# Re-ordering the first batch of an adaptive-norm transformer block: where component weights land, whose statistics come first, and who makes W_out's low parts

## The chip, the cores and the metric

The kernel runs on one core of a Trainium2 chip. The metric is the device time of one execution in microseconds (us), lower is better. The kernel before takes 377.56 us, the median of 3 runs (375.85 to 378.01).

## What is computed

Four batches of 512 tokens with 512 features, all in fp32. A conditioning vector gives six components of modulation; each batch goes through a modulated layer norm, an attention-like step and a feed-forward step. Cut to what matters here:

```
mod = (silu(c) @ wmod).reshape(B, 6, 1, -1)
sa, ca, ga, sb, cb, gb = (mod[:, i] for i in range(6))
ga = (2*(ga >= 0) - 1) * max(|ga|, 0.25)          # gb likewise
h  = layernorm(x) * (1 + ca) + sa
Xn = layernorm(h) * gamma + beta
Q, K, V = split(Xn @ W_in + b_in)
K, V = rotary(K), rotary(V)
A  = 0.5 * sum_over_tokens(cos_sim(K) * cos_sim(V)) + 0.5
x  = x + ga * ((A * Q) @ W_out + b_out + h)
h2 = layernorm(x) * (1 + cb) + sb
x  = x + gb * (relu(h2 @ W_up.T) @ W_down.T + (sum of top-2 softmax) * (h2 @ W_expert))
```

## The kernel before, in words

Every engine has its own program, written out by hand, and runs it strictly in order; semaphores tie them together. Tokens lie in tiles of 128 rows (four per batch, `t` 0 to 3) and features in chunks of 128 (four, `c` or `k`). A matrix product in fp32 accuracy is made of three products of a high part and a low part (`three`, L1175): the high part is a copy in `fp32r`, the low part is the remainder, one subtraction. So every operand has a "hi" copy, mostly on ScalarE (ACT) and a "lo" subtraction, mostly on VectorE (DVE) or GpSimd (POOL).

`PE` (TensorE) computes for batch 0: modulation rows (L1184, L1190), transposes of the normalised tile (`transposes0`, L1213), then `kv_tile(0, t)`: K and V of one row tile, 24 matmuls. Between tiles 1 and 2 stands `mod_rest` (L1196), which computes the other four components from four weight matrices of 1 MB at once, and after tile 2 `mod_turn` (L1207), which transposes them. Then come four feature chunks of Q (`feature_chunk`, twelve matmuls each) with the transposes of batch 1 between them, the four sums `a_sums` (L1259), `kv_tile(1, 0)`, and `out_rows_of(0)` (L1269), the product with W_out, which waits chunk by chunk for Q's low parts `g_lo` (`q_los`). Chunk 1 of Q shares a PSUM bank with the turned components and waits until DVE has read them (`mod_cols`, L1040, semaphore `col_sb`).

DVE carries in batch 0 (`first_attention`, L890): the layer-norm statistics, the bias rows of K and V (`kv_rows`), the rotary products (`kv_products`), the weighted sum over tokens (`kv_sum`), the low parts of the transposed tiles (`t0_split`, `t_split`), the rows `h` of batch 1 (`h_row`), `mod_gates` and `mod_cols`. Where it leaves batch 0 it makes `a_col` and `ab_col` (`a_evac`, L854), for which ACT's scaling of Q (`q_evac`, L603) waits, and after it `q_split` (L861).

ACT squares K and V for the norms (`norm_sums`, L529), normalises rows (`normalise`, `normalise_x`), and evacuates the transposes (`t0_evac`, `t_evac`). `kv_products(b, t)` on DVE waits for ACT's square of K.

POOL raises to the power -0.5 (`power`, `rstd_x`, `rstd_h`), makes low parts of weights (`low_kv`, `low_q`, `out_weight`), multiplies rows (`scale_rows`, L433) and adds the output bias to the rows h of batches 0 and 1 (`base`, L427, eight additions behind batch 0's sums).

`SP` issues every DMA on one queue in order. The weights of K and V come through the two halves of `stage`; a half is free again when its four low parts exist (`wlo_k`, `wlo_v`). The slots of `xs` that batches 2 and 3 will take hold the weights of the first two components at the start. Before, the four later component weights lie so:

```
MODS = ((2, x_slot(2)), (5, gate_bc[:]), (4, stage[:, 0, :]), (3, stage[:, 1, :]))
w_raw = (stage[:, 0, :], stage[:, 1, :], x_slot(3), stage[:, 0, :], stage[:, 1, :], ...)
```

## Time and profile before

| what | value |
|---|---|
| median of 3 runs | 377.56 us (375.85 to 378.01) |
| the profiled execution | 377.15 us, of which the span of the core is 375.1 us |
| PE busy | 353.0 us (94%) |
| DVE busy | 251.0 us (67%) |
| ACT busy | 165.9 us (44%) |
| POOL busy | 125.4 us (33%) |
| chain that ended last | PE 66%, DVE 13%, issue 10%, ACT 5%, POOL 3%, DMA 2% |

The table is an average over very different stages. PE is busy almost without a gap from about 75 us to the end; its idle time lies in the first 75 us, where DVE is busy nearly all the time. A row of the timeline gives the start, the duration of the group, the engine, the line and the operation, and in brackets the idle time before it with what ended it.

### The profile page before, as it was taken

Reading aid. Unit: us, or ns where it says so; the run is one execution under the profiler, and the core shown is the slowest. Engines: PE = TensorE matmul, PEld = TensorE weight load, DVE = VectorE, ACT = ScalarE, POOL = GpSimd, SP = SyncE. Lnnn points to the kernel's source line nnn. Section 1 sums busy time; section 2 is a strip of 40 time slices with the busy share of each in tenths; the row PEclk is TensorE's granted clock in tenths of the full one; section 3 lists DMA queues with packets and bytes.
Section 4 is the critical chain, followed back from the end, with each engine's and each line's share of the span. In section 5 each row is a group of like instructions: output and inputs, shape, how many; then the busy total and the mean of one; then the engine's idle time right before and its main releaser. Section 6 shows DMA issues by size and latency. Waiting matters only on the chain.

```text
span 375.1 us, 4910 instructions
## 1 busy us (share of the span) xinstructions
PE 353.0 (94%) x1776; PEld 287.6 (77%) x1776; DVE 251.0 (67%) x501; ACT 165.9 (44%) x317; POOL 125.4 (33%) x128
## 2 busy tenths in 40 slices
PE   3879797999998999989999999999999999999996
PEld 1238385788887888868888888988998898889885
DVE  2787999856978588885887458436812772383374
ACT  1476957772437811175305691246142604341110
POOL 0285745984932529325163151830010010000000
PEclk9969999989999999999999999999999999999999
DMA  6989567320030000000000002000200020011003
GB/s 199 389 319 315 221 223 243 141 121 2 1 84 0 2 0 16 14 1 2 0 28 2 0 0 114 21 10 28 87 0 0 30 84 2 0 58 57 0 2 113
DMA packets 10968, 27.45 MB, mean 73 GB/s; under 512 B 1200, under 2 KB 1584, under 8 KB 9792
## 3 DMA queue, kind: packets, MB, share of 16 engines
q1 hardware_dynamic: 10944, 27.13, 20.3%
q8 instruction: 14, 0.23, 0.2%
q14 instruction: 10, 0.08, 0.1%
HBM read 22.90 MB, written 4.23 MB: 72 GB/s over the span
## 4 chain that ended last, share of the span: by engine, by line
PE 66%; DVE 13%; issue 10%; ACT 5%; POOL 3%; DMA 2%; SPq 1%; POOLq 0%; DVEq 0%; ACTq 0%
PE ps L1177 21%; PE ps L1179 20%; PE ps L1178 20%; PE ps L1225 2%; DVE hb L771 2%; DMA xs<-in_X 2%; ACT sqj L536 1%; POOL hrs L383 1%; DVE hst L781 1%; ACT ps L599 1%; ACT z L587 1%; ACT t_hi L601 1%; PE ps L1190 1%; DVE prod L827 1%; DVE acc L841 1%
## 5 line engine op out<-in xcount | busy, mean ns | idle before, releaser
L1177 PE MATMUL ps<-wv_hi,t_hi 128*128 128x260 f32 (+1 forms) x192 | 62.2, 324 | 1.0 <-issue 0.6
L1178 PE MATMUL ps<-wv_lo,t_hi 128*128 128x260 f32 (+1 forms) x192 | 61.7, 322 | 0.0
L1179 PE MATMUL ps<-wv_hi,t_lo 128*128 128x260 f32 (+1 forms) x192 | 61.7, 321 | 0.0
L1177 PE MATMUL ps<-t_hi,w_hi 128*128 128x512 f32 x128 | 50.7, 396 | 2.4 <-DVE sb_col L1045 2.4
L1177 PE MATMUL ps<-w_hi,g_hi 128*128 128x512 f32 (+1 forms) x132 | 51.3, 389 | 0.0
L1179 PE MATMUL ps<-w_hi,g_lo 128*128 128x512 f32 (+1 forms) x132 | 50.6, 384 | 0.0
L1178 PE MATMUL ps<-w_lo,g_hi 128*128 128x512 f32 (+1 forms) x132 | 50.6, 383 | 0.0
L1179 PE MATMUL ps<-t_hi,w_lo 128*128 128x512 f32 x128 | 50.0, 391 | 0.0
L1178 PE MATMUL ps<-t_lo,w_hi 128*128 128x512 f32 x128 | 50.0, 390 | 0.0
L1177 PEld LDWEIGHTS ps<-wv_hi,t_hi 128*128 128x128 f32 x192 | 36.3, 189 | 4.8 <-issue 1.7
L1178 PEld LDWEIGHTS ps<-wv_lo,t_hi 128*128 128x128 f32 x192 | 36.4, 189 | 3.1
L1179 PEld LDWEIGHTS ps<-wv_hi,t_lo 128*128 128x128 f32 x192 | 36.4, 189 | 3.0
L383 POOL TENSOR_TENSOR hrs<-hve,expo 128x4 f32<-128x4 f32 (+2 forms) x12 | 11.5, 959 | 77.8 <-DVE hve L788 61.2
L1177 PEld LDWEIGHTS ps<-t_hi,w_hi 128*128 128x128 f32 x128 | 24.1, 188 | 7.6 <-DVE sb_col L1045 2.9
L536 ACT ACTIVATE sqj<-ps 128x512 bf16<-128x512 f32 x16 | 9.5, 593 | 44.8 <-DVE ps L810 37.7
L1177 PEld LDWEIGHTS ps<-w_hi,g_hi 128*128 128x128 f32 x132 | 24.8, 188 | 5.2 <-DVE g_lo L863 0.6
L1179 PEld LDWEIGHTS ps<-w_hi,g_lo 128*128 128x128 f32 x132 | 24.8, 188 | 5.0
L1178 PEld LDWEIGHTS ps<-w_lo,g_hi 128*128 128x128 f32 x132 | 24.8, 188 | 4.7
L354 POOL TENSOR_TENSOR rnm<-nsq,expo 128x2 f32<-128x2 f32 x16 | 11.5, 720 | 49.6 <-ACT sqj L536 49.6
L1179 PEld LDWEIGHTS ps<-t_hi,w_lo 128*128 128x128 f32 x128 | 24.0, 188 | 5.1
L1094 DVE SCALAR_TENSOR_TENSOR g_lo<-ps,g_hi 128x512 fp32r<-128x512 f32 x16 | 11.1, 692 | 24.9 <-ACT g_hi L616 24.8
L1178 PEld LDWEIGHTS ps<-t_lo,w_hi 128*128 128x128 f32 x128 | 24.1, 188 | 4.7
(151 smaller groups left out, 721.9 us busy)
## 6 DMA issues: line engine op xcount, KB each, us to landing
stage<-in_w SPq DMA_DIRECT2D x4, 1024.0 KB, 6.4
out<-xs SPq DMA_DIRECT2D x15, 256.0 KB, 2.0
xs<-in_X SPq DMA_DIRECT2D x3, 1024.0 KB, 9.1
xs<-in_wmod SPq DMA_DIRECT2D x8, 256.0 KB, 5.9
stage<-in_w SPq DMA_DIRECT2D x8, 256.0 KB, 8.2
stage<-in_wmod SPq DMA_DIRECT2D x2, 1024.0 KB, 9.8
gate_bc<-mod_rows SPq DMA_DIRECT2D x8, 256.0 KB, 3.3
xs<-in_X SPq DMA_DIRECT2D x2, 512.0 KB, 6.9
```

The costliest lines, as they stand in the source:

```text
L354: nc.gpsimd.tensor_tensor(dst, src, expo[:, 0:n], ALU.pow).then_inc(s, 1)
L383: nc.gpsimd.tensor_tensor(hrs[:, t0:t0 + n], hve[:, t0:t0 + n], expo[:, 0:n], ALU.pow).then_inc(hrs_s, n)
L536: nc.scalar.activation(sqj[:], src, ACT.Square, accum_out=nsq[:, t % 2, i:i + 1]).then_inc(nsq_s, 1)
L587: nc.scalar.activation(z[:, t, :], src, ACT.Identity, bias=hnm[:, t:t + 1], scale=hrs[:, t:t + 1]).then_inc(z_s, 1)
L599: nc.scalar.activation(whole, whole, ACT.Identity, bias=bias, scale=scale).then_inc(t_full, 1)
L601: nc.scalar.activation(t_hi[:, g % 2, c, :], whole, ACT.Copy).then_inc(t_his, 1)
L771: v.tensor_tensor(h, h, sa_bc[:], ALU.add).then_inc(h1_s, 1)
L1094: v.scalar_tensor_tensor(g_lo[:, c, :], ps[:, U_BANKS[c % 2], :], 0.0, g_hi[:, c, :].bitcast(f32), ALU.max, ALU.subtract).then_inc(u_los, 1)
L1177: mm(dst, l_hi, r_hi, start=start, stop=False)
L1178: mm(dst, l_hi, r_lo, start=False, stop=False)
L1179: return mm(dst, l_lo, r_hi, start=False, stop=stop)
L1225: last = nc.tensor.transpose(ps[:, T_BANKS[c % 2], t * P:(t + 1) * P], z[:, t, c * P:(c + 1) * P], idn[:])
```

## The change

It touches batch 0 alone, on all five queues. (1) Memory: component 4's weights go to slot 3 of `xs`, component 3's to the first half of `stage`, Q's weights to the second half, and the gates' rows are made in slot 3; so component 4 can be loaded without waiting for a low part, component 3 waits for K's, Q's weights for V's, and `load_x(3)` for `mod_turn`. (2) POOL: the second power for batch 0's own rows moves behind the first row's shift, the power for batch 1's x moves ahead of K's last low part, two of the `scale_rows` come before the first `weight`, and all `out_weight` copies come after the last `weight` of the batch. (3) DVE: batch 1's statistics are taken before those of row 3 of batch 0; inside `first_attention` the order of rows, sums and statistics changes; W_out's four low parts are now DVE's, behind the last transposed chunk and before `a_evac`. (4) ACT: `t0_evac(1)` goes ahead of a normalisation, the four normalisations of batch 1's x are spread between other work, and `normalise(1, 2, 2)` stands before `norm_sums(0, 2)`. (5) PE: `transposes0(3)` moves from the middle of tile 1 to its end.

```diff
@@ -87,3 +87,3 @@
         rows = v_sb[0:64, 0, :]
-        mod_raw, mod_abs, mod_sign, gate_rows = (stage[:, 1, i * D:(i + 1) * D] for i in range(4))
+        mod_raw, mod_abs, mod_sign, gate_rows = (xs[:, (3 * NT + i) * D:(3 * NT + i + 1) * D] for i in range(4))
         col = sb("col", [P, COLS])
@@ -259,6 +259,6 @@
 
-        MODS = ((2, x_slot(2)), (5, gate_bc[:]), (4, stage[:, 0, :]), (3, stage[:, 1, :]))
+        MODS = ((2, x_slot(2)), (5, gate_bc[:]), (4, x_slot(3)), (3, stage[:, 0, :]))
 
 
-        w_raw = (stage[:, 0, :], stage[:, 1, :], x_slot(3), stage[:, 0, :], stage[:, 1, :], stage[:, 0, :], stage[:, 1, :])
+        w_raw = (stage[:, 0, :], stage[:, 1, :], stage[:, 1, :], stage[:, 0, :], stage[:, 1, :], stage[:, 0, :], stage[:, 1, :])
 
@@ -305,3 +305,7 @@
 
-            sp.dma_start(MODS[1][1], wmod[MODS[1][0]]).then_inc(wm_in[MODS[1][0]], 16)
+            def load_component(i):
+                comp, weights = MODS[i]
+                sp.dma_start(weights, wmod[comp]).then_inc(wm_in[comp], 16)
+
+            load_component(1)
             sp.wait_ge(mod_sb, 1)
@@ -309,9 +313,9 @@
             sp.dma_start(mod_rows[ROW_SA], rows[32:32 + B, :]).then_inc(row_out, 16)
-            sp.dma_start(MODS[0][1], wmod[MODS[0][0]]).then_inc(wm_in[MODS[0][0]], 16)
+            load_component(0)
             sp.wait_ge(row_out, 32)
             load_modulation(1)
+            load_component(2)
             sp.wait_ge(wlo_k, NC)
-            sp.dma_start(MODS[2][1], wmod[MODS[2][0]]).then_inc(wm_in[MODS[2][0]], 16)
+            load_component(3)
             sp.wait_ge(wlo_v, NC)
-            sp.dma_start(MODS[3][1], wmod[MODS[3][0]]).then_inc(wm_in[MODS[3][0]], 16)
             sp.dma_start(w_raw[2], w[2]).then_inc(w_in[2], 16)
@@ -328,5 +332,5 @@
                              mod_rows[ROW_GA, b:b + 1, :].to_broadcast([P, D])).then_inc(ga_in, 16)
-            sp.wait_ge(wlo_q, NC)
-            load_x(3)
             sp.wait_ge(modt_ps, 1)
+            load_x(3)
+            sp.wait_ge(wlo_q, NC)
             sp.dma_start(w_raw[4], w[4]).then_inc(w_in[4], 16)
@@ -376,4 +380,2 @@
                 nc.gpsimd.tensor_copy(w_hi_of(WO, k), raw).then_inc(whi_out, 1)
-                pool.wait_ge(whi_out, k + 1)
-                nc.gpsimd.tensor_tensor(w_lo_of(WO, k), raw, w_hi_of(WO, k).bitcast(f32), ALU.subtract).then_inc(wlo_out, 1)
 
@@ -442,8 +444,6 @@
             def attention(b):
-                if b == 0:
-                    rstd_x(1)
                 weight(b, 0)
                 if b == 0:
-                    for t in range(NT):
-                        scale_rows(1, t)
+                    scale_rows(1, 2)
+                    scale_rows(1, 3)
                     weight(b, 1)
@@ -452,10 +452,8 @@
                         low_q(k)
-                    weight(b, 2)
                     rstd_h(1, 2, 2)
-                    out_weight(0)
+                    weight(b, 2)
                     rstd_x(2)
-                    out_weight(1)
                     weight(b, 3)
-                    out_weight(2)
-                    out_weight(3)
+                    for k in range(NC):
+                        out_weight(k)
                 else:
@@ -493,5 +491,5 @@
             rstd_x0(0)
-            rstd_x0(1)
             low_kv(0, 0)
             shift_h0(0)
+            rstd_x0(1)
             low_kv(1, 0)
@@ -501,5 +499,8 @@
             low_kv(1, 1)
-            shift_h0(3)
             low_kv(0, 2)
+            rstd_x(1)
             low_kv(0, 3)
+            scale_rows(1, 0)
+            shift_h0(3)
+            scale_rows(1, 1)
             for b in range(B):
@@ -571,8 +572,12 @@
 
+            def normalise_x1(t):
+                act.wait_ge(t_ps, t + 1)
+                act.wait_ge(xnm_s, 1)
+                nc.scalar.activation(z[:, t, :], xs[:, tok(1, t)], ACT.Identity, bias=xnm[:, t:t + 1],
+                                     scale=xrs[:, t:t + 1]).then_inc(xn_s, 1)
+
             def normalise_x(g):
-                wait(act, t_ps, g * NC if g > 1 else 0)
+                act.wait_ge(t_ps, g * NC)
                 act.wait_ge(xnm_s, g)
                 for t in range(NT):
-                    if g == 1:
-                        act.wait_ge(t_ps, t + 1)
                     nc.scalar.activation(z[:, t, :], xs[:, tok(g, t)], ACT.Identity, bias=xnm[:, t:t + 1],
@@ -628,6 +633,2 @@
             def first_attention():
-                norm_sums(0, 0)
-                normalise_x(1)
-                t0_evac(2)
-                t0_evac(3)
                 norm_sums(0, 1)
@@ -640,5 +641,5 @@
                 x_sums(2)
+                normalise(1, 2, 2)
                 norm_sums(0, 2)
                 x_squares(2)
-                normalise(1, 2, 2)
                 norm_sums(0, 3)
@@ -688,5 +689,12 @@
             nc.scalar.activation(rows, ps[0:64, MOD_BANK, :], ACT.Identity, bias=row_bias, scale=half[0:64, 0:1]).then_inc(mod_sb, 1)
-            normalise(0, 2, 1)
             t0_evac(1)
+            normalise(0, 2, 1)
+            normalise_x1(0)
+            normalise_x1(1)
+            t0_evac(2)
+            norm_sums(0, 0)
             normalise(0, 3, 1)
+            normalise_x1(2)
+            t0_evac(3)
+            normalise_x1(3)
             first_attention()
@@ -733,2 +741,8 @@
 
+            def split_lo_out(k):
+
+                dve.wait_ge(whi_out, k + 1)
+                v.tensor_tensor(w_lo_of(WO, k), w_raw[3][:, k * D:(k + 1) * D],
+                                w_hi_of(WO, k).bitcast(f32), ALU.subtract).then_inc(wlo_out, 1)
+
             def x_stats(g):
@@ -890,5 +904,2 @@
             def first_attention():
-                x_stats(1)
-                t0_split(1)
-                x_aggr(1)
                 dve.wait_ge(const_in, 32)
@@ -896,10 +907,7 @@
                 kv_rows(0, 0)
-                x_shift(1)
+                h_row(1, 0)
                 kv_products(0, 0)
+                h_row(1, 1)
                 kv_sum(0, 0)
-                h_row(1, 0)
-                kv_rows(0, 1)
                 t0_split(2)
-                h_row(1, 1)
-                t0_split(3)
                 h_stats(1, 0)
@@ -907,10 +915,10 @@
                 h_aggr(1, 0, 2)
+                kv_rows(0, 1)
+                t0_split(3)
+                h_row(1, 2)
                 kv_products(0, 1)
                 h_shift(1, 0, 2)
+                h_row(1, 3)
                 kv_sum(0, 1)
-                kv_rows(0, 2)
                 mod_gates()
-                h_row(1, 2)
-                h_row(1, 3)
-                x_mean(2)
                 h_stats(1, 2)
@@ -918,4 +926,6 @@
                 h_aggr(1, 2, 2)
-                kv_products(0, 2)
+                kv_rows(0, 2)
+                x_mean(2)
                 h_shift(1, 2, 2)
+                kv_products(0, 2)
                 kv_sum(0, 2)
@@ -924,4 +934,4 @@
                 x_var(2)
-                kv_products(0, 3)
                 t_split(1, 0)
+                kv_products(0, 3)
                 t_split(1, 1)
@@ -929,5 +939,7 @@
                 a_pairs(0)
-                x_shift(2)
                 t_split(1, 2)
                 t_split(1, 3)
+                x_shift(2)
+                for k in range(NC):
+                    split_lo_out(k)
 
@@ -1058,11 +1070,17 @@
             h_aggr0(1)
-            for t in (2, 3):
-                scale_row0(t)
-                h_row0(t)
-                if t == 3:
-                    t0_split(0)
-                h_stats(0, t)
-                h_aggr0(t)
+            scale_row0(2)
+            h_row0(2)
+            h_stats(0, 2)
+            h_aggr0(2)
+            scale_row0(3)
+            h_row0(3)
+            t0_split(0)
             split_lo_kv(1, 2)
+            x_stats(1)
+            x_aggr(1)
             split_lo_kv(1, 3)
+            t0_split(1)
+            x_shift(1)
+            h_stats(0, 3)
+            h_aggr0(3)
             first_attention()
@@ -1238,4 +1256,2 @@
                         transposes0(1)
-                    if b == 0 and t == 1 and k == 2:
-                        transposes0(3)
                     if b == 0 and k == 0:
@@ -1289,2 +1305,3 @@
                     if b == 0 and t == 1:
+                        transposes0(3)
                         mod_rest()
```

ACT in the middle of batch 0, from the normalisation of rows 0 and 1 of batch 1 on (`L536`/`L537` are the squares of `norm_sums`, `L587`/`L592` normalise); before:

```order
L587 ACTIVATE z<-hb,hnm,hrs 128x512 [waits t_ps,hnm_s]
L587 ACTIVATE z<-hb,hnm,hrs 128x512
L561 ACTIVATE xjunk,xsum<-xs 128x512 [waits x_in]
L561 ACTIVATE xjunk,xsum<-xs 128x512 [waits xsum_s] x3
L536 ACTIVATE sqj,nsq<-ps 128x512 [waits nsq_s,kb_s,rnm_s]
L536 ACTIVATE sqj,nsq<-v_sb 128x512 [waits nsq_s,kv_sb]
L569 ACTIVATE xjunk,xss<-xs,xmn 128x512 [waits xsum_s,xmn_s]
L569 ACTIVATE xjunk,xss<-xs,xmn 128x512 [waits xsum_s] x3
L587 ACTIVATE z<-hb,hnm,hrs 128x512 [waits hnm_s]
```

and now:

```order
L592 ACTIVATE z<-hb,hnm,hrs 128x512 [waits t_ps,hnm_s]
L592 ACTIVATE z<-hb,hnm,hrs 128x512
L562 ACTIVATE xjunk,xsum<-xs 128x512 [waits x_in]
L562 ACTIVATE xjunk,xsum<-xs 128x512 [waits xsum_s] x3
L592 ACTIVATE z<-hb,hnm,hrs 128x512 [waits hnm_s]
L592 ACTIVATE z<-hb,hnm,hrs 128x512
L537 ACTIVATE sqj,nsq<-ps 128x512 [waits nsq_s,kb_s,rnm_s]
L537 ACTIVATE sqj,nsq<-v_sb 128x512 [waits nsq_s,kv_sb]
```

The two normalisations of rows 2 and 3, which stood behind the squares of K and V of tile 2, now stand in front of them.

DVE at the end of batch 0 (`a_col`, `ab_col` are `a_evac`; `w_lo` is W_out's low part); before:

```order
L803 TENSOR_TENSOR t_lo<-ps,t_hi 128x512 [waits t_his] x2
L856 TENSOR_SCALAR a_col<-ps 128x4 [waits a_ps,ga_in]
L859 TENSOR_TENSOR ab_col<-a_col,col 128x4 [waits a_sb]
L863 TENSOR_TENSOR g_lo<-ps,g_hi 128x512 [waits q_his] x4
L810 TENSOR_TENSOR ps<-ps,bkv_bc 128x512 [waits kv_ps]
```

and now:

```order
L817 TENSOR_TENSOR t_lo<-ps,t_hi 128x512 [waits t_his] x2
L776 TENSOR_TENSOR xnm<-xmn,xrs 128x4 [waits xmn_s,xn_s,xrs_s]
L745 TENSOR_TENSOR w_lo<-stage,w_hi 128x512 [waits whi_out] x4
L870 TENSOR_SCALAR a_col<-ps 128x4 [waits a_ps,ga_in]
L873 TENSOR_TENSOR ab_col<-a_col,col 128x4 [waits a_sb]
L877 TENSOR_TENSOR g_lo<-ps,g_hi 128x512 [waits q_his] x4
```

Four subtractions from `stage` stand between the last transposed chunk and `a_col`.

POOL at the start (`xrs` is the power for x, `hrs` that for h, `w_lo` K's low part); before:

```order
L354 TENSOR_TENSOR xrs<-xve,expo 128x2 [waits xve_s,cst]
L354 TENSOR_TENSOR xrs<-xve,expo 128x2 [waits xve_s]
L386 TENSOR_TENSOR w_lo<-stage,w_hi 128x512 [waits whi_k]
L383 TENSOR_TENSOR hrs<-hve,expo 128x1 [waits hve_s]
L370 TENSOR_TENSOR hnm<-xmn,hrs 128x1 [waits nmu_s,hrs_s]
```

and now, with a later piece:

```order
L358 TENSOR_TENSOR xrs<-xve,expo 128x2 [waits xve_s,cst]
L388 TENSOR_TENSOR w_lo<-stage,w_hi 128x512 [waits whi_k]
L385 TENSOR_TENSOR hrs<-hve,expo 128x1 [waits hve_s]
L374 TENSOR_TENSOR hnm<-xmn,hrs 128x1 [waits nmu_s,hrs_s]
L358 TENSOR_TENSOR xrs<-xve,expo 128x2 [waits xve_s]
...
L388 TENSOR_TENSOR w_lo<-stage,w_hi 128x512 [waits whi_k]
L358 TENSOR_TENSOR xrs<-xve,expo 128x4 [waits h1_s,xve_s]
L388 TENSOR_TENSOR w_lo<-stage,w_hi 128x512 [waits whi_k]
```

The second power no longer stands before the first row's, and the power for batch 1 (`128x4`) stands before K's last low part.

## Rows read from the trace of the kernel before

**Rows 1.** Waits of PE up to 120 us: who waited for whom, total, times, longest

```profile
PE ps L1217 <- ACT z L587: 4.3, 1, 4.3
PE ps L1177 <- DVE sb_col L1045: 2.4, 1, 2.4
PE ps L1202 <- DMA stage<-in_wmod: 2.4, 1, 2.4
```

**Rows 2.** Stretches: length, busy us per engine, granted clock, DMA share, GB/s

```profile
core 0: us, PE busy (x) PEld busy (x) DVE busy (x) ACT busy (x) POOL busy (x), PEclk, DMA share, GB/s
20.25:27.20 6.95, 5.92 (x15) 2.42 (x16) 5.58 (x14) 6.38 (x12) 6.00 (x9) 0.52 0.86 345
59.80:62.25 2.45, 0.01 (x1) 0.00 (x0) 2.45 (x6) 1.68 (x4) 0.90 (x1) 1.00 0.79 171
75.10:78.50 3.40, 3.40 (x10) 2.68 (x9) 1.04 (x3) 3.34 (x7) 3.40 (x4) 0.51 0.80 325
27.00:28.00 1.00, 1.00 (x5) 0.76 (x4) 0.99 (x2) 0.45 (x1) 0.92 (x3) 0.82 0.04 12
```

**Rows 3.** Timeline of SP: component 3's weights are issued

```profile
30.65 0.43 SPq L316 DMA_DIRECT2D stage<-in_wmod  x1
```

**Rows 4.** Line 316 alone: its DMA's time to landing

```profile
DMA to landing us min/median/max: 10.8/10.8/10.8
```

**Rows 5.** Timeline of DVE, 27 to 63 us

```profile
27.61 2.47 DVE L737 BATCH_NORM_STATS2 xst<-xs 128x6 f32<-128x512 f32 x4
...
35.68 0.29 DVE L827 TENSOR_TENSOR prod<-prod 128x128 f32<-128x128 f32 x1
36.00 0.43 DVE L829 TENSOR_TENSOR prod<-prod,rot_sb 128x256 f32<-128x256 f32 x1
...
38.07 1.77 DVE L771 TENSOR_TENSOR hb<-hb,sa_bc 128x512 f32<-128x512 f32 x1
...
58.80 0.70 DVE L827 TENSOR_TENSOR prod<-prod 128x128 f32<-128x128 f32 x1
59.53 1.45 DVE L829 TENSOR_TENSOR prod<-prod,rot_sb 128x256 f32<-128x256 f32 x1
...
62.04 0.17 DVE L1045 COPY sb_col<-ps 128x16 f32<-128x16 f32 x1
```

**Rows 6.** Timeline of ACT, 61 to 76 us

```profile
61.09 1.52 ACT L587 ACTIVATE z<-hb,hnm,hrs 128x512 f32<-128x512 f32 x2 [0.77 <-DVE hnm L792]
62.89 0.60 ACT L536 ACTIVATE sqj<-ps 128x512 bf16<-128x512 f32 x1 [0.28 <-issue]
...
75.72 0.72 ACT L609 ACTIVATE ps<-ps,ab_col,a_col 128x512 f32<-128x512 f32 x1
```

**Rows 7.** Timeline of POOL, 17 to 127 us

```profile
17.58 0.70 POOL L354 TENSOR_TENSOR xrs<-xve,expo 128x2 f32<-128x2 f32 x1 [6.11 <-DVE xve L1008]
...
32.07 1.01 POOL L354 TENSOR_TENSOR xrs<-xve,expo 128x4 f32<-128x4 f32 x1 [1.83 <-DVE xve L744]
...
36.44 5.77 POOL L440 TENSOR_TENSOR hb<-z,ca_bc 128x512 f32<-128x512 f32 x4
...
72.78 9.98 POOL L431 TENSOR_TENSOR hb<-hb,bo_bc 128x512 f32<-128x512 f32 x8 [0.43 <-DVE pair L852]
...
122.07 5.04 POOL L431 TENSOR_TENSOR hb<-hb,bo_bc 128x512 f32<-128x512 f32 x4 [3.97 <-DVE pair L852]
```

**Rows 8.** Timeline of DVE, 72 to 126 us

```profile
72.70 1.27 DVE L803 TENSOR_TENSOR t_lo<-ps,t_hi 128x512 fp32r<-128x512 f32 x2
...
74.86 0.46 DVE L859 TENSOR_TENSOR ab_col<-a_col,col 128x4 f32<-128x4 f32 x1
...
80.92 0.69 DVE L863 TENSOR_TENSOR g_lo<-ps,g_hi 128x512 fp32r<-128x512 f32 x1 [0.58 <-ACT g_hi L612]
...
95.05 3.47 DVE L771 TENSOR_TENSOR hb<-hb,sa_bc 128x512 f32<-128x512 f32 x2
...
124.56 1.31 DVE L859 TENSOR_TENSOR ab_col<-a_col,col 128x4 f32<-128x4 f32 x1
```

**Rows 9.** Timeline of PE: chunk 3 of W_out's first row tile begins

```profile
83.69 0.39 PE L1177 MATMUL ps<-w_hi,g_hi 128*128 128x512 f32 x1
```

More of the change, by code:

```diff
@@ L328, in _ @@
                              mod_rows[ROW_GA, b:b + 1, :].to_broadcast([P, D])).then_inc(ga_in, 16)
+            sp.wait_ge(modt_ps, 1)
+            load_x(3)
             sp.wait_ge(wlo_q, NC)
-            load_x(3)
-            sp.wait_ge(modt_ps, 1)
             sp.dma_start(w_raw[4], w[4]).then_inc(w_in[4], 16)
@@ L452, in attention @@
                         low_q(k)
+                    rstd_h(1, 2, 2)
                     weight(b, 2)
-                    rstd_h(1, 2, 2)
-                    out_weight(0)
                     rstd_x(2)
-                    out_weight(1)
                     weight(b, 3)
-                    out_weight(2)
-                    out_weight(3)
+                    for k in range(NC):
+                        out_weight(k)
                 else:
@@ L501, in _ @@
             low_kv(1, 1)
+            low_kv(0, 2)
+            rstd_x(1)
+            low_kv(0, 3)
+            scale_rows(1, 0)
             shift_h0(3)
-            low_kv(0, 2)
-            low_kv(0, 3)
+            scale_rows(1, 1)
             for b in range(B):
@@ L688, in _ @@
             nc.scalar.activation(rows, ps[0:64, MOD_BANK, :], ACT.Identity, bias=row_bias, scale=half[0:64, 0:1]).then_inc(mod_sb, 1)
+            t0_evac(1)
             normalise(0, 2, 1)
-            t0_evac(1)
+            normalise_x1(0)
+            normalise_x1(1)
+            t0_evac(2)
+            norm_sums(0, 0)
             normalise(0, 3, 1)
+            normalise_x1(2)
+            t0_evac(3)
+            normalise_x1(3)
             first_attention()
@@ L918, in first_attention @@
                 h_aggr(1, 2, 2)
+                kv_rows(0, 2)
+                x_mean(2)
+                h_shift(1, 2, 2)
                 kv_products(0, 2)
-                h_shift(1, 2, 2)
                 kv_sum(0, 2)
@@ L924, in first_attention @@
                 x_var(2)
+                t_split(1, 0)
                 kv_products(0, 3)
-                t_split(1, 0)
                 t_split(1, 1)
```

## The prediction

> **What bounds the kernel now.** I read the waits of PE first, then the timelines of the engines that ended them, then the granted clock. PE is the bound from about 75 us on, so a change in batch 0 is worth what it does to the moment at which PE gets through batch 0 and into W_out's product. There PE waits three times [rows 1]: 4.3 us for the first normalised tile, 2.4 us before `mod_rest` for component 3's weights, 2.4 us in chunk 1 of Q for `sb_col`, the last write of `mod_cols`. Two stretches run at half the full clock, the lower of its two levels (1.2 of 2.4 GHz) [rows 2]: 20.25 to 27.20, after the 4.3 us wait, and 75.10 to 78.50, behind the four sums. The third wait stands apart from the other two. DVE is busy for the whole 2.45 us of it [rows 2], and it is busy nearly without a gap from 33 us on: `mod_cols` ends at 62.21 (62.04 + 0.17) [rows 5] because DVE's queue is that long, not because PE or a DMA is late. So the point to ask about in batch 0 is when DVE reaches `mod_cols`, and the next when it reaches `a_evac`.
>
> One more reading matters. DVE instructions with two tensors in SBUF take longer when POOL works beside them. The same multiplication takes 0.43 us at 36.00 and 1.45 us at 59.53, its neighbour 0.29 and 0.70 [rows 5]; adding 512 columns takes 1.77 us beside POOL's `scale_rows` [rows 5, 7] and 3.47 us for two at 95.05 [rows 8]; and `ab_col`, four columns, takes 1.31 us beside `base` [rows 7, 8]. A low part of a transposed chunk, with one operand in PSUM, takes 1.27 us for two with `base` running (0.64 each) [rows 8]. It looks as if such a DVE instruction waits until POOL's current one is over, and POOL's next for it.
>
> **The change part by part.** All sums are made against the profiled execution's 377.15 us (span 375.1), which is 0.41 under the median of 377.56; that is less than the runs scatter, and I leave it. Some 0.5% (1.9 us) is about what a measurement of this kernel tells from no change.
>
> *The start.* POOL's second power, which began at 17.58 and had waited 6.11 us, stood in front of the first row's [rows 7]; now the first row's shift is free of it, and most of 2 us of PE's 4.3 us wait should go. But K's last low part now stands behind batch 1's power (1.01 us [rows 7]), which needs batch 1's statistics, 2.47 us on DVE [rows 5]; that low part then comes at about the time at which PE used it before. What PE wins in front of tile 0 it waits for at chunk 3 of tile 0. I book 0; the ends are -1.0 (the low part is early) and +0.6 (it is late).
>
> *The DMAs.* Component 3's weights were issued at 30.65 and landed 10.8 us later [rows 3, 4], 41.45, when PE had waited 2.4 us. In 27 to 28 us the DMA engines were nearly idle (share 0.04) [rows 2], since the queue waited for the modulation rows. With those rows ready earlier, component 2, the broadcasts, component 4 and component 3 follow each other without that gap, and component 3 lands 2 to 3 us earlier. The wait before `mod_rest` goes. Its worth at the end is 0 all the same: PE only reaches chunk 1 of Q earlier, and there it waits for DVE's `mod_cols`, which needs nothing of it so early. What is late next is DVE. As a bound from below, all 2.4 us would count if DVE were ahead. Q's weights and `load_x(3)` move too; both land before their users, at no cost.
>
> *The way to `mod_cols`.* DVE has the same work in front of it as before. Gained: W_out's subtractions on POOL no longer stand beside `kv_products(0, 2)`, 1.02 us of the multiplication and 0.41 of its neighbour, 1.4 us [rows 5]. Lost: `kv_products(0, 2)` waits for ACT's square of K, and ACT now first has to normalise rows 2 and 3 of batch 1, which itself waits for DVE's shift just ahead. So DVE stands for one pair of normalisations, 1.52 us, and one square, 0.60 us, with its reading and the hand-overs some 2.3 us [rows 6]. Before, the square was done long ahead. Net +0.9: `mod_cols` at 63.1 and not 62.2. Likewise the square of tile 0 comes behind an evacuation; I put that in the range with 0.6. Ends: -1.4 (ACT's order hides behind something) and +2.5.
>
> *The clock.* PE gets to chunk 1 of Q 2.4 us earlier (57.4) and can go on at 63.1: 5.7 us without a matmul. After 4.3 us of that the granted clock was at half for 6.95 us; the 2.45 us of 59.80 to 62.25 left it at full [rows 2]. 5.7 is nearer the first. The later stretch at half lasted 3.4 us, with PE dense; half of it, 1.7 us, is lost, and chunk 1 lies before the transposes on which everything up to `a_sums` hangs. I take +1.7; ends 0 and 3.4. From chunk 1 to the sums I leave the 11.3 us of before.
>
> *W_out's low parts.* POOL loses four subtractions off the path; it was not waited for there. DVE gets four, between the last transposed chunk (73.97 before) and `a_evac`. Their cover is thin: `ab_col` was ready at 75.32, 1.35 after that chunk; ACT began the scaling at 75.72, so 0.4 is free; the last `g_lo` ended at 81.61 and PE opened chunk 3 at 83.69, 2.1 free [rows 6, 8, 9]. Together 3.85 us. `base` starts right behind the sums and runs for 9.98 us [rows 7], so all four subtractions, which read `stage` and the high part from SBUF, run beside it. At 1.74 each (half of 3.47) they take 7.0, less 0.6 for the first, which meets POOL in the middle; `a_col` 0.16 and `ab_col` 1.31 [rows 8] follow. 7.9 - 3.85 = +4.0 us. Undisturbed at 0.64 each, with `ab_col` as before, it would be 3.2 and cost nothing: ends 0 and +4.6. I take 4.0 since the neighbour of the same shape and operand places is the addition at 95.05. Queued behind the four are `ab_col`, Q's evacuation on ACT, all four `g_lo`, and PE's W_out product.
>
> The notes speak for this part of the change: the Trainium skill, GPSIMD Engine Reference, section 4.1 Engine selection, says to put an elementwise operation of two inputs on VectorE, as GpSimd is about twice as slow at it. By it the term is 0 and the sum 379.8; by the rows it is 383.8. Singly the rule holds here; beside a busy GpSimd the rows show nothing of it.
>
> Sum: 0 + 0 + 0.9 + 1.7 + 4.0 = +6.6; 377.15 + 6.6 = **383.8 us**.
>
> **The rivals.** (a) *The subtractions fit, and the time falls.* If the four take less than 0.8 us each (3.85 - 0.62 = 3.2 in all), `a_evac` costs nothing; if also the 1.4 us beside POOL is gained and the normalisations on ACT are covered, `mod_cols` comes at 60.8, chunk 1 starts 1.4 earlier, and the half-clock stretch of 75 to 78.5 may be absent, 1.7: 377.15 - 3.1 = 374.0. For it: DVE is busy for only 1.04 of the 3.40 us from 75.10 [rows 2] and has room; the single durations. Against it: the rows of two SBUF operands beside POOL. Chance 0.20. This is where the engine-selection rule (by that rule, the subtractions at about their undisturbed length) would lead. (b) *Only W_out's parts cost.* `mod_cols` is on time and the clock stays: 377.15 + 4.0 = 381.2. For it: the stall of 2.45 us left the clock alone. Against: PE arrives earlier, so the wait is longer even so. Chance 0.25. (c) *Nothing that counts.* The DMA gain reaches the end in part and pays for W_out's parts: 377.2. Chance 0.10. (d) My forecast, 0.45.
>
> **How the numbers follow.** The point is (d). Cases (b) and (d) are slower: 0.70. Case (c) is within 0.5%: 0.10. Case (a) is faster: 0.20. The low end, 375.0, takes in (c), (b) and the upper part of (a), down to where its gains are 2.2 and not 3.1; the rest of (a), about 0.12, is left out. The high end adds 0.6 for a late start, 0.6 for W_out's upper bound, the clock's other 1.7 and most of a microsecond at `mod_cols`: 387.5, with under 0.1 above. The range of (b) and (d) alone is 380 to 387.5.
>
> **What would show it.** In the timeline of DVE, `w_lo<-stage` four times for about 7 us in all beside `base`, and `ab_col` over 1 us: W_out's term; under 3.2 us refutes it. In PE's waits, `stage<-in_wmod` gone, `sb_col` at 5 to 6 us, and a new wait for `g_lo` in W_out's product. In ACT's, the square of K of tile 2 behind `z`, and DVE idle before `cross` for about 2 us. In the windows, a granted clock near 0.5 behind the `sb_col` wait. I am wrong as a whole if PE opens chunk 3 of W_out's first tile before 84 us.

## The result, and the profile after the change

The changed kernel takes 382.21 us (median of 4 runs, 380.48 to 383.9) against 377.37 us (median of 4, 375.85 to 378.01) for the kernel before: ratio 1.0124, 95% interval 1.0075 to 1.0172. It is slower by 1.2%, and the interval leaves out 1. The profiled execution took 382.35 us with a span of 380.3; the one before had a span of 375.1, so 5.2 us are to be found between the two traces.

PE's longest waits after the first weights, of the changed kernel (who waited for whom, total, times, longest), over the whole span; they answer to [rows 1]:

```profile
PE ps L1195 <- DVE sb_col L1057: 4.2, 1, 4.2
PE ps L1243 <- DVE t_lo L817: 3.2, 5, 1.0
PE ps L1195 <- DVE g_lo L877: 2.8, 2, 2.5
PE ps L1195 <- DVE t_lo L812: 2.8, 1, 2.8
PE ps L1235 <- ACT z L592: 2.0, 1, 2.0
PE ps L1195 <- POOL w_lo L388: 0.8, 1, 0.8
```

The wait for component 3's weights is gone; the one for `sb_col` is longer; `g_lo` (in W_out's product) and two at tile 0 are new. Three stretches of the changed kernel, as in [rows 2]: the wait ahead of chunk 1 of Q, what follows it, and a piece of W_out's product.

```profile
core 0: us, PE busy (x) PEld busy (x) DVE busy (x) ACT busy (x) POOL busy (x), PEclk, DMA share, GB/s
58.09:62.28 4.19, 0.00 (x1) 0.00 (x0) 3.15 (x10) 4.00 (x12) 1.13 (x2) 0.98 0.84 256
62.28:65.70 3.42, 3.42 (x8) 2.72 (x9) 1.22 (x3) 2.03 (x6) 2.04 (x4) 0.52 1.05 425
86.00:89.20 3.20, 3.20 (x9) 1.84 (x8) 2.53 (x4) 1.76 (x4) 0.00 (x0) 0.50 0.36 58
```

Before, chunk 1 ran at the full clock. The half-clock stretch behind the sums (75.10 to 78.50 in [rows 2]) is gone from its place, and one of 3.2 us has come at 86 us, behind the wait for `g_lo`.

DVE's timeline of the changed kernel, 33 to 88 us, for [rows 5, 8]:

```profile
33.48 0.70 DVE L824 TENSOR_TENSOR ps<-ps,bkv_bc 128x512 f32<-128x512 f32 x1 [0.76 <-PE ps L1197]
...
36.61 0.29 DVE L833 TENSOR_TENSOR cross<-ps,v_sb 128x128 f32<-128x128 f32 x1 [1.14 <-ACT sqj L537]
...
42.83 1.19 DVE L802 TENSOR_SCALAR hve<-hmv 128x2 f32<-128x2 f32 x1
...
47.32 0.28 DVE L838 TENSOR_TENSOR prod<-cross 128x128 f32<-128x128 f32 x1
47.52 0.28 DVE L841 TENSOR_TENSOR prod<-prod 128x128 f32<-128x128 f32 x1
47.84 0.42 DVE L843 TENSOR_TENSOR prod<-prod,rot_sb 128x256 f32<-128x256 f32 x1
...
49.95 2.05 DVE L855 SCALAR_TENSOR_TENSOR acc<-prod,wgt,acc 128x768 f32<-128x768 f32 x1
...
58.95 0.29 DVE L833 TENSOR_TENSOR cross<-ps,v_sb 128x128 f32<-128x128 f32 x1 [2.23 <-ACT sqj L537]
...
62.06 0.17 DVE L1057 COPY sb_col<-ps 128x16 f32<-128x16 f32 x1
...
68.70 0.69 DVE L817 TENSOR_TENSOR t_lo<-ps,t_hi 128x512 fp32r<-128x512 f32 x1 [5.20 <-ACT t_hi L606]
...
75.08 5.79 DVE L745 TENSOR_TENSOR w_lo<-stage,w_hi 128x512 fp32r<-128x512 f32 x4
80.98 1.05 DVE L873 TENSOR_TENSOR ab_col<-a_col,col 128x4 f32<-128x4 f32 x1
...
87.36 0.69 DVE L877 TENSOR_TENSOR g_lo<-ps,g_hi 128x512 fp32r<-128x512 f32 x1 [0.58 <-ACT g_hi L617]
```

`sb_col` is written at 62.06, where it was before (62.04), although DVE now stands idle for 1.14 and 2.23 us until ACT has made two squares. W_out's four low parts take 5.79 us, and the last `g_lo` comes 6.4 us later than in [rows 8]. Taken one by one (shortest, median and longest in ns), the first of the four is short, and the others are not:

```profile
L745 DVE TENSOR_TENSOR w_lo<-stage,w_hi x4: 679/1780/1785, 75.1 to 79.1; 128x512 fp32r<-128x512 f32 x4
```

POOL's timeline (`base` is the last row), and PE's at chunks 0 and 3 of W_out's first row tile and the start of the second:

```profile
29.00 1.39 POOL L358 TENSOR_TENSOR xrs<-xve,expo 128x4 f32<-128x4 f32 x1 [3.50 <-DVE xve L758]
...
48.04 6.82 POOL L388 TENSOR_TENSOR w_lo<-stage,w_hi 128x512 fp32r<-128x512 f32 x4 [0.16 <-ACT w_hi L528]
...
73.85 11.85 POOL L433 TENSOR_TENSOR hb<-hb,bo_bc 128x512 f32<-128x512 f32 x8 [6.10 <-DVE pair L866]
```

```profile
84.29 0.50 PE L1195 MATMUL ps<-w_hi,g_hi 128*128 128x512 f32 x1 [2.52 <-DVE g_lo L877]
...
88.28 0.63 PE L1195 MATMUL ps<-w_hi,g_hi 128*128 128x512 f32 x1
...
89.52 0.39 PE L1195 MATMUL ps<-w_hi,g_hi 128*128 128x512 f32 x1
```

Chunk 3 opens at 88.28 against 83.69 [rows 9]; the second row tile begins at 89.52, 5.15 us later than before (84.37). From there the two kernels run alike, so the whole loss is made by then. It splits at the four sums, which began at 73.53 before and at 75.16 now: 1.6 us ahead of them, 3.5 behind.

### The profile page after: what moved, and what is told of

It reads as the page before. It is cut to its first block, busy times and chain, and to the rows that moved or that the text cites. A ratio compares the mean times of both kernels' runs of the same rounds, so it can differ in the third digit from the quotient of the medians.

```text
span 380.3 us, 4913 instructions
## 1 busy us (share of the span) xinstructions
PE 354.9 (93%) x1776; PEld 288.4 (76%) x1776; DVE 251.9 (66%) x505; ACT 166.1 (44%) x317; POOL 122.2 (32%) x124
## 4 chain that ended last, share of the span: by engine, by line
PE 63%; DVE 16%; issue 9%; ACT 5%; POOL 5%; DMA 1%; POOLq 0%; SPq 0%; DVEq 0%; ACTq 0%
PE ps L1195 20%; PE ps L1197 19%; PE ps L1196 19%; PE ps L1202 2%; PE ps L1243 2%; POOL w_lo L388 2%; POOL hrs L385 1%; DVE hst L795 1%; ACT sqj L537 1%; DVE w_lo L745 1%; DMA xs<-in_wmod 1%; DVE hst L789 1%; ACT ps L604 1%; DVE acc L852 1%; DVE t_lo L817 1%
## 5 line engine op out<-in xcount | busy, mean ns | idle before, releaser
L1195 PE MATMUL ps<-t_hi,w_hi 128*128 128x512 f32 x128 | 51.5, 402 | 4.2 <-DVE sb_col L1057 4.2
L1195 PE MATMUL ps<-w_hi,g_hi 128*128 128x512 f32 (+1 forms) x132 | 52.2, 395 | 2.8 <-DVE g_lo L877 2.8
L1195 PE MATMUL ps<-w_hi,t_hi 128*128 128x512 f32 x64 | 26.2, 410 | 3.6 <-DVE t_lo L812 2.8
L817 DVE TENSOR_TENSOR t_lo<-ps,t_hi 128x512 fp32r<-128x512 f32 x28 | 19.0, 689 | 15.3 <-ACT t_hi L606 15.2
L537 ACT ACTIVATE sqj<-ps 128x512 bf16<-128x512 f32 x16 | 9.5, 592 | 44.0 <-DVE ps L824 37.2
```

Of the source, the lines that this page charges most:

```text
L537: nc.scalar.activation(sqj[:], src, ACT.Square, accum_out=nsq[:, t % 2, i:i + 1]).then_inc(nsq_s, 1)
L817: v.tensor_tensor(t_lo[:, g % 2, c, :], ps[:, T_BANKS[c % 2], :], t_hi[:, g % 2, c, :].bitcast(f32), ALU.subtract).then_inc(t_los, 1)
L1195: mm(dst, l_hi, r_hi, start=start, stop=False)
```

## Experiments

The kernel before had a median of 375.98 to 376.15 us on the chips of these runs. Ratios are to it, with 95% intervals. Since starts differ by up to a microsecond between executions, I read the traces by two marks: when `a_sums` begins, and what is left of the span from there. A table of both stands behind the experiments.

**W_out's low parts on POOL again.**

```diff
                 nc.gpsimd.tensor_copy(w_hi_of(WO, k), raw).then_inc(whi_out, 1)
+                pool.wait_ge(whi_out, k + 1)
+                nc.gpsimd.tensor_tensor(w_lo_of(WO, k), raw, w_hi_of(WO, k).bitcast(f32), ALU.subtract).then_inc(wlo_out, 1)
...
-                for k in range(NC):
-                    split_lo_out(k)
```

> The changed kernel with W_out's four low parts made on POOL again, right behind their casts. If those four on VectorE are most of the loss (my account of the changed kernel's trace: 5.2 us are fixed by 93 us, of which 1.6 at a_sums and the rest behind it), ab_sb comes 1.3 to 2 us behind the last t_lo, the new g_lo wait of PE goes, and the time falls by 3.5 to 378.8 us. If the loss was made ahead of a_sums instead (DVE and ACT order, clock), the time stays within 1 us of 382.3. The stretch at half clock that the changed kernel moved to 86 us should come back at 75 to 79 us.

380.6 us, ratio 1.0111 (1.0079 to 1.0142): neither number. The rest behind `a_sums` fell from 305.1 to 299.9 us, but `a_sums` came at 79.24, 4 us later. The wait of 4.20 us ahead of chunk 1 was followed here by a longer stretch at half the clock, and the subtractions on POOL now stood beside `kv_products(0, 3)`, with `t_split(1, 1)` behind it. PE waited for that `t_lo` and fell to the half clock once more. The window and PE's row of this kernel:

```profile
61.80:67.90 6.10, 5.43 (x13) 4.17 (x14) 1.89 (x6) 2.67 (x8) 3.98 (x6) 0.50 0.85 329
```

```profile
74.42 0.66 PE L1243 MATMUL ps<-idn,z 128*128 128x128 f32 x4 [2.16 <-DVE t_lo L819]
```

So the undoing moved a contention from behind the sums to ahead of them. It doesn't isolate the term.

**The kernel before with only the four subtractions moved to DVE** (out of `out_weight`, the same `split_lo_out`, called behind `t_split(1, 3)`).

> The kernel before with only W_out's four subtractions moved to VectorE, behind the last t_lo; nothing else changed. My forecast's term: 4 x 1.45 to 1.74 us beside base, ab_col over 1 us, +4.0, so 381.2 us. The rival that they fit into idle time (under 0.8 us each): 377.2 us. A second theory, that the loss of the changed kernel comes from its order of norms ahead of a_sums, also says 377 to 378 here.

> The same kernel as before_lows_dve, for a trace that can be compared: by the comparison it is 2.7 us slower than the kernel before. With the subtractions beside base at 1.4 to 1.5 us each, ab_col over 1 us and ab_sb at about 81 us, the last g_lo comes 5 us later than before and PE waits for it; the time 378.9 to 381.2 us. If they are at 0.65 each and the loss lies elsewhere, ab_sb comes at 78.

First comparison: 378.93 us, 1.0071 (1.0045 to 1.0097); its profiled execution took 1235.84 us, and its trace can't be set against the others. Second, on another chip: 381.32 us (2 runs), 1.0143 (1.0070 to 1.0217). My 381.2 lies between what the two ratios give with 377.15, 379.8 and 382.5. Both are slower than the kernel before, the first by less than the term of 4.0 (2.7 us) and the second by more (5.4). The second trace shows the mechanism as forecast, on DVE and at PE:

```profile
73.87 6.63 DVE L735 TENSOR_TENSOR w_lo<-stage,w_hi 128x512 fp32r<-128x512 f32 x4
80.61 1.03 DVE L863 TENSOR_TENSOR ab_col<-a_col,col 128x4 f32<-128x4 f32 x1
```

```profile
83.89 0.80 PE L1183 MATMUL ps<-w_hi,g_hi 128*128 128x512 f32 x1 [3.63 <-DVE g_lo L867]
```

`a_sums` came at 73.66, where it is in the kernel before. The loss is all behind it.

**Contention or length.** The same number of instructions on DVE, with `base` held back:

```diff
                     pool.wait_ge(bo_in, 16)
+                    pool.wait_ge(wlo_out, NC)
```

> The changed kernel, with POOL's base held until all four low parts are written; the number of instructions on VectorE stays the same. If what costs is POOL's work beside them (contention), each subtraction takes 0.6 to 0.7 us, ab_col 0.1, ab_sb is written at 78 us and not 82, and the time falls by about 3.5 to 378.8 us, unless base, now ending near 88 us, is late for o_evac (then 380). If it is the mere number of instructions ahead of a_evac, each still takes about 1.45 us and the time stays at 382.3 us.

378.75 us, ratio 1.0069 (1.0042 to 1.0095). DVE's and POOL's rows:

```profile
75.40 2.49 DVE L746 TENSOR_TENSOR w_lo<-stage,w_hi 128x512 fp32r<-128x512 f32 x4
78.00 0.16 DVE L874 TENSOR_TENSOR ab_col<-a_col,col 128x4 f32<-128x4 f32 x1
```

```profile
78.12 10.11 POOL L433 TENSOR_TENSOR hb<-hb,bo_bc 128x512 f32<-128x512 f32 x8 [9.97 <-DVE w_lo L746]
```

The four take 2.49 us in place of 5.79, and the four-column product 0.16 in place of 1.05; the rest behind `a_sums` falls by 3.8 us. Nothing on DVE was changed. Length alone is refuted: what costs is `base` beside them, and `base` 4.3 us later is not missed.

**The order of DVE** (`kv_products(0, 3)` ahead of `t_split(1, 0)`, as before).

> The changed kernel with VectorE's t_split(1, 0) back behind kv_products(0, 3), as before. If the order is what makes a_sums 1.6 us late (kv_products(0, 3) waits behind a t_hi that comes only at 68.7), a_sums moves from 75.16 to 73.6 and the time falls by 1.5 to 380.8 us. If chunk 1 of Q at half clock (62.4 to 65.7 us) is the cause, PE's transposes and so t_hi and t_lo come as late as now, a_sums stays at 75 and the time within 0.5 us of 382.3.

383.03 us, 1.0166 (1.0120 to 1.0211). By the time both theories miss; by the trace the order counts. From the start of chunk 1 to the sums it took 11.7 us (63.53 to 75.21) and not 12.9 (62.28 to 75.16), both at half clock. But everything came a microsecond later. POOL's first `scale_rows` waited for a broadcast that landed 2.3 us later than in the changed kernel's trace (35.74 against 33.45), and DVE then waited 2.42 us for POOL's row. The trace is of an execution of 383.47 us; the four runs lie between 380.37 and 383.69, so the time tells little here. POOL's row:

```profile
35.74 1.29 POOL L442 TENSOR_TENSOR hb<-z,ca_bc 128x512 f32<-128x512 f32 x1 [4.46 <-DMA sa_bc<-mod_rows]
```

**The order of ACT.**

```diff
-                normalise(1, 2, 2)
                 norm_sums(0, 2)
+                normalise(1, 2, 2)
                 x_squares(2)
```

> The changed kernel with ScalarE's norm_sums(0, 2) ahead of normalise(1, 2, 2); x_squares(2) stays behind both. VectorE's wait of 2.2 us ahead of kv_products(0, 2) should go, sb_col come near 60 and not at 62.1, PE's wait ahead of chunk 1 of Q fall from 4.2 to about 2 us and leave the clock at full, so a_sums comes 2.2 + 1.6 us earlier: 378.5 us. If only the wait counts and the clock falls all the same: 380.2. If VectorE's idle time there is not on the path: 382.3 us.

378.77 us, ratio 1.0082 (1.0054 to 1.0111). `sb_col` at 59.78, PE's wait 2.10 us, the clock full behind it, `a_sums` at 71.41: 3.75 us earlier, where 3.8 were expected.

**Chunk 0 twice**, to fill PE's wait with work:

```diff
                     if b == 0 and c == 1:
+                        for k in range(NC):
+                            three(ps[:, Q_BANKS[0], :], w_hi_of(WQ, k)[:, 0:P], w_lo_of(WQ, k)[:, 0:P],
+                                  t_hi[:, 0, k, :], t_lo[:, 0, k, :], k == 0, k == NC - 1)
                         pe.wait_ge(col_sb, 2)
```

> The changed kernel with chunk 0 of Q computed twice on PE (12 more matmuls, 2.7 us, the same result), which fill PE's wait of 4.2 us ahead of chunk 1. Nothing else moves. If the idle time is what takes the clock to half in 62.4 to 65.7 us, the granted clock stays at 1 there with a wait of 1.5 us, the transposes behind chunk 1 start about 1.7 us earlier and the time falls by 1.0 to 1.7, to 381 us, although PE has more to do. If the clock falls for another reason, the time stays at 382.3 or rises.

380.26 us, 1.0115 (1.0068 to 1.0163). The wait and what follows it:

```profile
60.52:62.00 1.48, 0.01 (x2) 0.00 (x1) 1.33 (x5) 1.42 (x5) 0.14 (x1) 1.00 0.72 192
62.00:65.40 3.40, 3.40 (x17) 2.85 (x18) 1.22 (x3) 2.04 (x6) 2.03 (x4) 1.00 1.05 422
```

PE gets through chunk 1's twelve matmuls and into the transposes here (17 in all) in the time of 8 of the twelve in the changed kernel. From chunk 1 to the sums: 11.4 us (62.00 to 73.38) against 12.9. That is the price of the clock with this order of DVE, 1.5 us.

**The placement and the DMA order alone**, in the kernel before (component 4 in x's fourth slot, component 3 in `stage`'s first, Q's weights in its second; queue order as in the change).

> The kernel before with only the change's placement of component weights, modulation rows and Q's weights, and its order on the DMA queue; every engine's order is as before. Component 3 should land about 2 us earlier and the wait before mod_rest go. If VectorE's way to mod_cols is the bound, as I forecast, PE waits 2.4 us longer ahead of chunk 1 of Q instead, and the time is the same as the kernel before (376.0 us), or 1.7 more where that longer wait takes the clock to half. If the rival holds that the gain at the DMA reaches the end, it is 373.6 us.

375.71 us, 0.9996 (0.9969 to 1.0024): the same. In its profiled execution PE still waited 3.0 us for component 3, and `sb_col` was written at 62.52. So no gain was made at the DMA, and this run cannot test what one is worth. It shows the reverse. Behind that wait `mod_rest` ran at about half the clock (0.57), PE began tile 2 at 46.81 and not 45.23, and 1.6 us of PE's lead were gone without a cost: PE waited 1.3 us for `sb_col` in place of 2.4. The window of `mod_rest` in this run:

```profile
42.30:45.90 3.60, 3.60 (x24) 1.25 (x20) 3.46 (x12) 2.29 (x3) 1.70 (x4) 0.57 0.05 18
```

Why the wait stayed can be read from the queue. Component 2's weights are issued ahead of components 4 and 3, in this run (first row) and in the changed kernel (second):

```profile
27.40 0.36 SPq L310 DMA_DIRECT2D xs<-in_wmod  x1
```

```profile
24.61 0.36 SPq L308 DMA_DIRECT2D xs<-in_wmod  x1
```

Component 3 was issued at 30.27 and landed 11.0 us later here; in the changed kernel it was issued at 31.65 and landed 6.6 us later. Counted from component 2's issue these are 13.9 and 13.6 us, and in the kernel before 14.0 (27.44 to 41.45). Component 2 goes out right behind the modulation rows, which PE makes behind its wait for `z`: 5.1 us here, 4.3 before, 2.0 in the changed kernel. All nine traces with the new start are without the wait for component 3, and the four comparable ones with the old start have it (2.4 to 4.9 us), this one with the new placement among them. So the wait went with the new start, and the placement alone does not remove it. Whether the start alone would, no run shows.

**The three orders together** (base behind the low parts, products first, sums first), and then also `mod_cols` behind `mod_gates`, alone in the kernel before and with the three:

```diff
                 mod_gates()
+                mod_cols()
...
                 kv_sum(0, 2)
-                mod_cols()
```

> The changed kernel with base behind the low parts, t_split(1, 0) behind kv_products(0, 3), and norm_sums(0, 2) ahead of normalise(1, 2, 2). If the three causes add (3.6 for base, 1.2 for the order of products, 2.2 to 3.9 for the sums and the clock): 382.3 - 7 to 8.7, so 374 to 375.5 us, under the kernel before. If the wait saved at one place comes back at the next (PE waiting for t_hi or for g_lo), about 378 us.

> The kernel before with VectorE's mod_cols (0.25 us) right behind mod_gates, instead of behind kv_sum(0, 2); the turned rows are there from 51.5 us. PE's wait of 2.4 us ahead of chunk 1 goes. If PE is then held at chunk 2 by kv_products(0, 3), which comes as late as ever, 1.1 to 1.5 us are left of it and the time falls to 374.7 us; if the whole of it comes back there or at the last t_lo, 376.0 us; if all of it counts, 373.5.

> three_together with mod_cols right behind mod_gates. PE's wait of 2.1 us ahead of chunk 1 goes, and with it the half clock of 60.5 to 64 us; chunk 2 waits for kv_products(0, 3), done near 63.8 us, about 2 us. a_sums comes 1.5 us earlier (70.3), and the time is 373.9 us. If PE's wait only moves and the clock falls at its new place: 375.4 us as without it.

Three together: 375.43 us, 0.9982 (0.9954 to 1.0011), the same as the kernel before; the causes add, nearly to the amount expected. `mod_cols` early in the kernel before: 376.43 us, 1.0012 (0.9987 to 1.0037). The wait ahead of chunk 1 went, and came back: PE waited 1.67 us for the last `t_lo` ahead of the sums (0.93 before), in an execution in which component 3 also came 0.9 us later, `mod_rest` ran at a clock of 0.57, and DVE stood for 5.98 us until PE had K of tile 2. That execution took 378.0 us, and the ten runs fall into five of 375.1 to 375.6 and five of 377.3 to 378.15. So the trace does not show what the early `mod_cols` is worth there; the times show nothing clear of noise. With the three orders it counts: 373.29 us, 0.9923 (0.9894 to 0.9951), against 0.9982 without it, and the clock stays at full from 60 us to the sums. This version beats both kernels.

**W_out's low parts in DVE's gaps** (calls between `kv_products(0, 3)` and `t_split(1, 3)`, `base` free, `x_var(2)` behind `kv_products(0, 3)`, ACT and `mod_cols` as in the best version).

> The changed kernel with the same orders as three_cols_early, but W_out's low parts not behind the last t_lo: two behind kv_products(0, 3), one behind t_split(1, 0), one behind t_split(1, 2), all ahead of a_sums, where VectorE has 2.8 us of idle time and POOL is not at base; base starts freely, and x_var(2) stands behind kv_products(0, 3). If the place beside base is the whole price of the four, ab_sb comes within 1.5 us of the last t_lo and the time is 373.5 us or a little under. If the four delay the t_lo instead, 375 to 376 us.

379.0 us, ratio 1.0069 (1.0041 to 1.0096). Both cases missed. With `x_var` later, POOL's casts of W_out came later too, and DVE stood for them ahead of `t_split`; PE waited 6 us for the `t_lo` and then ran at half clock. DVE's row, and PE's wait and the stretch behind it:

```profile
68.06 2.08 DVE L745 TENSOR_TENSOR w_lo<-stage,w_hi 128x512 fp32r<-128x512 f32 x2 [2.60 <-POOL w_hi L380]
```

```profile
64.81:70.80 5.99, 0.00 (x1) 0.00 (x1) 3.35 (x7) 1.83 (x3) 5.00 (x7) 0.79 0.45 183
70.80:75.00 4.20, 4.11 (x13) 3.27 (x14) 4.13 (x8) 2.59 (x4) 1.06 (x1) 0.50 0.00 0
```

**The two marks of all traces** (us; the last column is the span less the start of `a_sums`):

| kernel | wait ahead of chunk 1 | clock behind it | `a_sums` | from there to the end |
|---|---|---|---|---|
| four low parts on DVE beside `base`: | | | | |
| changed | 4.2 | half | 75.2 | 305.1 |
| before_lows_dve_again | 0.4 | full | 73.7 | 305.8 |
| products3_first | 4.2 | half | 75.2 | 306.3 |
| sums2_first | 2.1 | full | 71.4 | 305.3 |
| chunk0_twice | 1.5 | full | 73.4 | 304.6 |
| not beside it: | | | | |
| before | 2.4 | full | 73.5 | 301.6 |
| lows_on_pool | 4.2 | half | 79.2 | 299.9 |
| base_behind_lows | 4.2 | half | 75.6 | 301.3 |
| three_together | 2.1 | half | 71.8 | 302.1 |
| components_alone | 1.3 | full | 74.0 | 300.1 |
| before_cols_early | none | full | 74.5 | 301.6 |
| three_cols_early | none | full | 69.8 | 301.7 |
| lows_spread | none | full | 76.7 | 300.7 |

The last column falls into two groups that don't overlap, with means of 305.4 and 301.1.

## Why the prediction was right, step by step

The forecast was 383.8 us by a sum of +6.6; the profiled execution came at 382.35, +5.2. The places were right, one term was wrong and one a little large.

*W_out's low parts, +4.0.* The two groups of the table give 4.3; the two traces, 3.5 from the sums to W_out's second row tile. The price of one was right: three of the four took 1.78 us, where 1.74 was forecast. The first took 0.68, although `base` was already running, so the four took 5.79 us and not 6.4, and `ab_col` took 1.05 and not 1.31. That it is contention and not length is shown by base_behind_lows. The Trainium skill's GPSIMD Engine Reference has both sides: its section 4.1 Engine selection calls VectorE about twice as fast at such an operation, and singly the runs agree (2.49 us for four against 1.27 to 1.41 us for each of POOL's in the kernel before). Its section 8 Key points says that the two engines contend where a VectorE instruction has two SBUF inputs. At 1.78 us beside `base` the advantage of the first rule is gone. Rival (a), where that rule would lead, is refuted.

*The clock at chunk 1, +1.7.* It fell, and cost 1.5 us by chunk0_twice. That the size fits is in part luck, as the next term shows. The wait was 4.2 us and not the 5.7 forecast, since `mod_cols` was not late and PE arrived at 58.1 and not at 57.4.

*From chunk 1 to the sums, unchanged 11.3.* With the full clock it is 11.4 in two traces with the new order of DVE. At half clock the new order takes 12.9 and the old one 11.7 to 11.8 (products3_first, three_together). With the old order the same fall of the clock would have cost some 0.4 us (11.7 against 11.3). So `t_split(1, 0)` ahead of `kv_products(0, 3)` costs nothing by itself, but lets the clock's loss through: DVE waits 5.2 us for a `t_hi` with a product behind it that was ready long before. I had costed that move at nothing, and named no cover for it.

*`mod_cols`, +0.9.* This step failed: "DVE has the same work in front of it as before", and the gain of 1.4. It came at +0.02. The wait for the square is 2.23 us as forecast (2.3), and the first one, put in the range with 0.6, 1.14. What I missed lies mostly on the gain's side: I had moved one POOL neighbour in the sum and not looked for the others. `low_q` on POOL, which stood beside `kv_products(0, 1)`, now starts behind it (48.04 us), and `scale_rows` is spread out. In the kernel before, the last three instructions of those products and POOL's `low_q` were:

```profile
45.98 1.36 DVE L824 TENSOR_TENSOR prod<-cross 128x128 f32<-128x128 f32 x1
47.27 1.38 DVE L827 TENSOR_TENSOR prod<-prod 128x128 f32<-128x128 f32 x1
48.68 1.40 DVE L829 TENSOR_TENSOR prod<-prod,rot_sb 128x256 f32<-128x256 f32 x1
```

```profile
45.90 5.33 POOL L386 TENSOR_TENSOR w_lo<-xs,w_hi 128x512 fp32r<-128x512 f32 x4
```

Now the three take 0.28, 0.28 and 0.42. Counted from start to start, from `kv_rows(0, 0)` to `sb_col`, DVE gained 3.2 us there, 1.2 in `kv_products(0, 2)`, 1.6 in the rows `h` (the two of 1.77 and 1.19 us before take 0.68) and 0.2 elsewhere: 6.2. It lost 3.1 standing idle (3.37 for 0.32), 1.0 in `kv_sum(0, 1)` (2.05 for 1.01), 1.0 in `hve` (1.19 for 0.17), 0.4 in `mod_gates` and 0.1 elsewhere: 5.7. With a start 0.5 us later, nothing is left. The mechanism is that of W_out's term, but that the two sides cancel so closely is luck.

*The start, 0.* K and V of tile 0 ended 0.5 us later (`kv_rows` at 33.48, before 32.95), within its ends. PE's wait for `z` fell from 4.3 to 2.0 us, and waits of 2.8 and 0.8 us took its place.

*The DMAs, 0.* Right. Component 3 landed at 38.3 us and not 41.45, with the earlier rows as forecast. PE ended chunk 0 at 58.09 and not 59.80, and waited that much longer for an `sb_col` that came at the same moment. components_alone (0.9996) shows the other direction: a later PE costs nothing there either.

Of the rivals, (b), only W_out's parts, had 381.2 us, and the median of 382.21 is nearer to it (1.0) than to the forecast (1.6). Its `mod_cols` on time came true as well. The times don't separate the two. The traces do: the clock fell, and 1.6 us were lost ahead of the sums. Of "What would show it", `sb_col` at 5 to 6 us and 7 us for the four were too high; the rest is there.

Open: what the new start is worth alone, and the share of the DVE order in the full time of the changed kernel, since products3_first was late at its start for another reason.

## What to carry to other kernels

Before moving an elementwise instruction with two SBUF operands to DVE, look at what POOL does in the same microseconds: behind one another beside a POOL loop of such instructions, each went at POOL's pace (1.78 us, where one addition of `base` took up to 1.81). A single one of four columns took anything from 0.23 us (lows_spread) over 0.46 (the kernel before) and 1.05 to 1.31 [rows 8], all beside `base`. It is not only instructions of two tensors: `hve`, one tensor of two columns, took 1.19 us beside a `scale_rows`. Where both are needed, hold the one with slack: a single wait on POOL (base_behind_lows, 378.75 us) was worth more than undoing the move (lows_on_pool, 380.6). And undo pieces of a bundled change one at a time in the trace, marked at a common event, since an order that costs nothing at full clock may cost a microsecond at half.

## What the runs showed of the hardware

*A fall of the clock is not settled by the wait alone.* The same wait of 2.10 us, sums2_first (first two rows) and three_together (last two), with the same instructions ahead of it on PE:

```profile
57.90:60.00 2.10, 0.00 (x1) 0.00 (x1) 1.91 (x7) 2.07 (x5) 0.68 (x2) 1.00 0.87 296
60.00:63.40 3.40, 3.40 (x17) 2.83 (x18) 1.31 (x3) 3.24 (x10) 1.01 (x1) 1.00 0.82 249
```

```profile
57.96:60.06 2.10, 0.00 (x1) 0.01 (x1) 1.91 (x7) 2.07 (x5) 0.68 (x2) 1.00 0.89 318
60.06:63.50 3.44, 3.44 (x9) 2.77 (x10) 2.04 (x6) 3.26 (x10) 1.01 (x1) 0.58 0.79 281
```

One ran on at 2.4 GHz (1.00), the other fell to 1.2 GHz for most of the stretch. Of the waits ahead of chunk 1, those of 1.5 us or less left the clock at full and all of 4.2 us brought it down; at 2.1 to 2.4 us both occurred. Ahead of `mod_rest` a wait of 2.42 us (the kernel before) left it at full, and waits of 2.99 us (components_alone) and 3.76 us (before_cols_early) did not (0.57 behind both). At the sums, a wait of 0.92 us in components_alone left it at full where 0.93 us in the kernel before did not. From the sums to the end these two took 300.1 and 301.6 us. The kernel before scatters over 374.6 to 378.4 us; such falls may be a part of it, which no run here separates.

*One execution with PE at a third of its speed.* In before_lows_dve's profiled execution PE was busy for 1225 us of a span of 1233.8, with matmuls of 1.1 us where 0.39 is usual, while DVE's instructions took their usual 0.68 us; the granted clock in the records was 1.000 throughout. The kernel's four other runs took 378.55 to 379.02 us.
